# A table that places the maxima pieces inside each step of a four-stage transformer kernel

## The reference, cut to what matters

```python
scores = jnp.einsum('bhqd,bhkd->bhqk', query, key) / np.sqrt(D_K)      # 16 heads, 512 x 1601
scores = jnp.where(mask == 0, jnp.float32(-1000000000.0), scores)
attn = jax.nn.softmax(scores, axis=-1)
x = jnp.einsum('bhqk,bhkd->bhqd', attn, value)
```

## Time and profile before

| | |
|---|---|
| median of 3 runs | 2892.51 us (2891.18 to 2892.61) |
| profiled execution, span from the first to the last instruction | 2889.1 us |
| what the median has beyond that span | 3.4 us |
| TensorE busy by the profile | 2692.4 us, 93% |
| VectorE busy | 1738.0 us, 60% |
| ScalarE busy | 1458.0 us, 50% |
| mean granted clock of TensorE | 0.985 |

### The profile page before, as it was taken

One profiled execution on the slowest core, in us unless ns is written; L12 is line 12 of the kernel. 1 busy time (PEld: TensorE's weight loads), 2 busy tenths in 40 slices (PEclk: granted clock), 3 DMA queues, 4 the chain that ended last, 5 costly groups with the idle time before them and its releaser, 6 DMA issues.

```text
span 2889.1 us, 39579 instructions
## 1 busy us (share of the span) xinstructions
PE 2692.4 (93%) x13707; PEld 1286.5 (45%) x13707; DVE 1738.0 (60%) x4231; ACT 1458.0 (50%) x2923; POOL 281.4 (10%) x344
## 2 busy tenths in 40 slices
PE   7878999999999999999999999999999989879998
PEld 3533433343334433443334343533353323239998
DVE  3346676667766776577666766676666768641111
ACT  2232565546554656456545755565546556633332
POOL 1200200010001100020002000200010000002222
PEclk8988999999999999999999999999999999999999
DMA  5431312323132313241224032422322032039995
GB/s 180 124 102 42 100 42 77 91 76 81 32 108 75 100 41 108 53 121 42 88 56 131 18 107 60 107 50 68 99 62 63 18 83 47 10 115 369 375 375 208
DMA packets 215141, 296.37 MB, mean 103 GB/s; under 512 B 50533, under 2 KB 180813, under 8 KB 214934
## 3 DMA queue, kind: packets, MB, share of 16 engines
q1 hardware_dynamic: 198428, 221.50, 27.3%
q0 software_dynamic: 16512, 72.32, 7.3%
HBM read 232.87 MB, written 60.50 MB: 102 GB/s over the span
## 4 chain that ended last, share of the span: by engine, by line
PE 79%; DVE 8%; ACT 6%; issue 5%; DMA 2%; SPq 1%; POOL 0%; ACTq 0%; POOLq 0%; DVEq 0%
PE PS L1462 12%; PE PS L1418 11%; PE PS L1445 10%; PE PS L1104 6%; DVE mxC L1984 6%; PE PS L1079 6%; PE PS L1644 5%; PE PS L1656 5%; PE PS L1133 3%; PE PS L1306 3%; PE PS L1200 2%; ACT reg L970 2%; PE PS L1223 2%; PE PS L1092 2%; PE PS L1215 2%
## 5 line engine op out<-in xcount | busy, mean ns | idle before, releaser
L970 ACT ACTIVATE reg<-PS 128x512 f32<-128x512 f32 (+1 forms) x1664 | 971.9, 598 | 962.5 <-PE PS L1445 956.8
L1984 DVE TENSOR_REDUCE mxC<-PS 128x1 f32<-128x400 f32 (+1 forms) x2048 | 1097.1, 570 | 560.8 <-PE PS L1418 548.0
L1418 PE MATMUL PS<-reg 96*128 96x400 bf16 (+1 forms) x2048 | 669.1, 340 | 64.2 <-DVE mxC L1984 39.4
L1445 PE MATMUL PS<-reg 99*128 99x512 bf16 (+1 forms) x1664 | 613.1, 384 | 38.0 <-ACT reg L970 29.5
L1418 PEld LDWEIGHTS PS<-reg 96*128 96x128 bf16 x2048 | 194.7, 97 | 585.2 <-DVE mxC L1984 452.4
L1462 PE MATMUL PS<-reg 128*17 128x512 f32 (+1 forms) x3328 | 440.0, 601 | 0.3 <-DVE reg L2008 0.3
L1445 PEld LDWEIGHTS PS<-reg 99*128 99x128 bf16 (+1 forms) x1664 | 163.2, 100 | 383.7 <-ACT reg L970 237.4
L1104 PE MATMUL PS<-reg 128*128 128x512 f32 (+1 forms) x416 | 211.6, 601 | 0.4 <-ACT reg L844 0.4
L1079 PE MATMUL PS<-reg 128*128 128x512 f32 (+1 forms) x512 | 208.8, 522 | 1.0 <-ACT reg L871 0.7
L1016 ACT ACTIVATE reg<-PS,reg 128x128 f32<-128x128 f32 x312 | 89.3, 369 | 217.3 <-PE PS L1644 217.3
L1644 PEld LDWEIGHTS PS<-reg 128*128 128x128 f32 x1248 | 147.8, 194 | 3.1 <-issue 1.0
(11 more groups left out here) (233 smaller groups left out, 2552.9 us busy)
## 6 DMA issues: line engine op xcount, KB each, us to landing
reg<-in_D_W SPq DMA_DIRECT2D x78, 1024.0 KB, 9.3
reg<-in_A_mask POOLq DMA_DIRECT2D x32, 800.5 KB, 5.7
dramK<-reg SPq DMA_DIRECT2D x144, 100.0 KB
dramV<-reg SPq DMA_DIRECT2D x48, 272.0 KB, 3.1
reg<-in_ctxT POOLq DMA_DIRECT2D x8, 1601.0 KB, 8.8
reg<-in_ctx POOLq DMA_DIRECT2D x8, 1536.0 KB, 7.7
dramQ<-reg SPq DMA_DIRECT2D x96, 128.0 KB
reg<-dramQ SPq DMA_DIRECT2D x32, 384.0 KB, 6.4
```

The lines of the kernel that those rows point to most:

```text
L970: act.activation(pr[u % RING][0:r, :], PS[0:r, s_bank(v), :], ACT.Exp).then_inc(a_expC, 1)
L1418: last = mm(PS[:, bank, 0:w], qs[(NG * bb + g) % 3][0:ROWS, h, t * P:(t + 1) * P], ks[g % 2][0:ROWS, h, c0:c0 + w], start=True, stop=True)
L1445: last = mm(PS[0:r, bank, :], ks[g % 2][0:STK, h, c * P:c * P + r], qs[(NG * b + g) % 3][0:STK, h, :], start=True, stop=not with_mask)
L1984: v.tensor_reduce(mxC[:, h, t, j:j + 1], PS[:, m_ring(bb, g)[i % len(m_ring(bb, g))], 0:M_CH[j][1]], AX.X, ALU.max).then_inc(v_mx, 1)
```

## The change

The table of four rows becomes one of four periods: batch 0, batches 1 to 5, batch 6, batch 7. Each has a row for each group, and an entry for each step. The digits of an entry say how many pieces `piece()` issues at its first, second, third call in the step. On VectorE the number of pieces in a step follows the new table, but `piece()` there still takes one at each call. All groups now begin in step 3, group 3 among them; the last piece lies in step 43 or 44. 64 pieces for each group, their order and their banks stay.

```diff
-PIECES = ("0001212322232223211111210112221321001111113300000000",
-          "0002203232320132102231233322111111031002110100000000",
-          "0001001211031002110222133323330021330113312300000000",
-          "0000000000032223311121332223311121221122211320000000")
+PIECES = (
...
+    ("0 0 0 1 01 11 01 011 1 01 101 012 0 0111 01 111 011 01 11 011 01 1 01 011 1 0 0 01 1 011 1 11 011 011 101 02 011 0 011 01 111 0 11 11 0111 0 0 0 0 0 0 0",
+     "0 0 0 1 021 1 011 02 01 1 011 11 0 1 012 01 112 0 021 02 012 0 021 02 021 01 0 111 1 1 0 02 01 1 1 02 1 01 1 11 01 0 11 021 0 0 0 0 0 0 0 0",
+     "0 0 0 11 02 0 01 02 01 1 1 011 0 11 01 02 01 0 0 111 0 01 0 11 021 111 1 01 111 111 1 01 111 1 012 01 1 012 0 02 111 1 01 0121 1 0 0 0 0 0 0 0",
+     "0 0 0 1 022 0 01 11 0 1 0211 02 01 012 01 02 021 1 001 02 0 0 112 11 01 111 11 01 112 0 1 11 0 1 01 02 01 0 1 11 1 0 0 112 02 0 0 0 0 0 0 0"),
...
+     "0 0 0 1 0 3 0 13 1 1 0 13 1 1 0 13 1 1 1 03 1 1 1 03 1 1 1 03 1 1 1 04 0 1 1 13 0 1 1 13 0 1 1 13 1 0 0 0 0 0 0 0"),
...
+def period(b):
+
+    return {0: 0, B - 2: 2, B - 1: 3}.get(b, 1)
+
+
+def slots(b, g, v):
+
+    return [int(d) for d in PIECES[period(b)][g].split()[v]]
+
+
+def chunks(b, g, v):
+
+    upto = [sum(int(d) for step in PIECES[period(b)][g].split()[:w] for d in step) for w in (v, v + 1)]
     return range(*upto)
...
                 g, v = u // UN, u % UN
                 if g < NG - 1:
-                    return (b, g + 1, chunks(g, v)) if 0 <= b < B else (b, g + 1, ())
-                return (b + 1, 0, chunks(g, v)) if 0 <= b + 1 < B else (b + 1, 0, ())
+                    return b, g + 1, chunks(b, g, v)
+                return (b + 1, 0, chunks(b, g, v)) if b + 1 < B else (b + 1, 0, ())
...
-                todo = iter(ahead)
+                todo, counts = iter(ahead), iter(slots(b, g, v))
 
                 def piece():
-                    for i in todo:
-                        scores_c(nb, ng, i, with_mask)
-                        break
+                    for _ in range(next(counts, 0)):
+                        scores_c(nb, ng, next(todo), with_mask)
```

More of the change, by code:

```diff
@@ L60 @@
 MT = (47, 46, 47, 47)
-PIECES = ("0001212322232223211111210112221321001111113300000000",
-          "0002203232320132102231233322111111031002110100000000",
-          "0001001211031002110222133323330021330113312300000000",
-          "0000000000032223311121332223311121221122211320000000")
+PIECES = (
[16 rows of a table added]
+)
 U_O1, U_O2, U_LD, U_XD, U_GATE = (8, 10), (13, 16), 18, (28, 30), 33
@@ L123, in rows @@
     return P if c < CT - 1 else CL
-def chunks(g, v):
-    upto = [sum(int(d) for d in PIECES[g][:w]) for w in (v, v + 1)]
+def period(b):
[4 more added lines that the diff above has]
+    upto = [sum(int(d) for step in PIECES[period(b)][g].split()[:w] for d in step) for w in (v, v + 1)]
     return range(*upto)
```

## The result

The changed kernel takes 2959.11 us (median of 4 runs, 2957.81 to 2960.84) against 2892.56 for the kernel before on the same chip: **slower, ratio 1.0232, 95% interval 1.0217 to 1.0246**, some 67 us. The forecast was 2922.5, its range ended at 2952, and the time lies above it. The profiled execution has a span of 2956.7 us, 67.6 more than before, so its stretches can be set against the rows of before directly. Lines of the code moved: on TensorE by 24 (`scores_c` is L1442, `scores_t` L1469, `transpose_m` L1456, `project_k` L1157), on VectorE by 23 (`maxima` is L2007), on GpSimd and SyncE by 24.

A forecast was written before the change was run, and what follows sets the result against it. TensorE was taken to bound the batches. Terms -10.0 + 2.5 + 1.7 + 8.8 + 2.2 = +5.2 us for each of batches 0 to 5, with batches 6 and 7 together +30: 2892.5 + 30 = 2922.5 us, range 2889 to 2952.

The forecast's parts named there:

- What bounds the kernel: Batches: TensorE, busy for 93% of the span; its waits are time, other engines' only if TensorE stands behind them.
- Group 3's stall: Group 3, step 3: the first piece waits 10.1 us for the next batch's queries; net +8.8 us a batch, 8.5 to 10.
- the path hangs on work ahead of step 155, which the change leaves alone: Queries' load in group 3: the landing stays some 14.1 us behind the group's start.
- The clock: TensorE behind group 3's stall: half clock for 4.0 to 8.8 us, losing 2.0 to 4.4; +2.2 us a batch taken.
- VectorE's order: VectorE's list: the prediction notes that reduces move between steps, and gives this no term in the sum.
- Pieces spread out: TensorE's pieces, all groups: two of one bank stay 1.0 us apart, so spreading gains 10.0 us a batch, 6.6 to 11.5.
- Short steps left bare: Steps with fewer pieces: waits ahead of `scores_t` grow from 3.0 to 5.3 us a batch; +2.5 taken, 0 to +4.
- the group's end: `transpose_m` waits for the split behind later last pieces: some 1.1 us in group 1, 0.6 in group 0; +1.7 a batch.
- Batches 6 and 7: Last two batches: batch 6 +1.1 us, its stall growing from 5.3 to some 10.7; batch 7 -2 us.
- The first: Rival, whole kernel: the pieces' waits outweigh stall and clock, 11.0 us a batch; not slower, 2867 at 14 us; chance 0.17.
- the pieces' bound: TensorE's pieces: the spread gains at most some 11.5 us a batch.
- The third: Rival, whole kernel: other waits take up every piece's wait, leaving the stall alone, +71 us, 2964; chance 0.06.

The follow-up runs named there:

- e3: The changed kernel with 32 matmuls, their product unused, on TensorE ahead of group 3's wait for the queries; ratio 1.0176 to the kernel before.
- e1: The changed kernel with the old counts in group 3, one piece at each place; groups 0 to 2 keep the new rows; ratio 1.0051 to the kernel before.
- e5: e1 with VectorE's reduces behind all its other work of their step, in all four groups; ratio 1.0009 to the kernel before.
- e6: e1 with the same number of pieces in every step, but one at each place from the first on; ratio 0.9968 to the kernel before.
- e12: e11 plus a group 3 row for batches 0 to 5, spread from step 11 by measured streaming time; ratio 0.9992 to the kernel before.
- e11: e6 with the old counts in batch 7; ratio 0.9952 to the kernel before.
- e10: The kernel before, with the mask load issued ahead of group 3's queries cut to 8 columns; 2880.2 us in a single run, 2891.6 before.

## Why the prediction was right, and where it failed

**What bounds the kernel**: right. By the profile 64 of the 67 us are TensorE's idle time; its busy time grew by 3 us, and that of VectorE and ScalarE fell.

**Group 3's stall**: right in kind, and near in size. The place, the idle first piece and its cause are as forecast, and e3 names the load. The step "the path hangs on work ahead of step 155, which the change leaves alone" was not quite true: a mask load on GpSimd's queue, which I had not listed among the things that stand behind the stall, moves behind the queries, and the stall is 8.1 us, not 10.1. Group 3 as a whole grew by 8.6 to 10.0 us in batches 0 to 3, by the forecast 9.0, but there the second fall of the clock is in it; in batches 4 and 5, without that, by 7.0 and 7.2. So that its +51.1 comes near the forecast +54 is in part luck: a stall that was shorter and a fall of the clock that was not in the sum.

**The clock**: right in kind. 2.2 us for each stall became 2.3, but a second fall behind 1.2 us of idle time, in four batches, was not in the sum; e3 measures 16 us for all of it, 13 forecast. The shorter time that the Trainium skill gives in "TensorE: Matmul & The Clock Gate", "HAM oscillation" (1.67 us throttled for each wait of its example) is not what the rows show: 4.6 us at half clock in batch 3.

**VectorE's order, priced at nothing: the step that failed.** The prediction notes "on VectorE it moves reduces between steps" and gives that no term. I laid out TensorE's list alone and held each piece to 1.0 us behind the one two before it, whatever VectorE was doing. But the diff names places on TensorE only, and VectorE goes through its list in the old order: a piece that TensorE makes late in its step stops what stands behind its reduce there, as `rest_k` at 1260.47. What that costs is the difference between e1 and e5, in which only VectorE's order differs: 23.1 us in groups 0 to 2 of batches 0 to 5, 3.9 a batch. With it gone these groups are 1.8 us a batch below before; with it they are 1.6 above in the changed kernel, where the forecast had -3.8. It shows as the waits ahead of `project_k`, `scores_t` and the transposes, which grew by more than the pieces' waits fell. e1 against e6 gives the same price from the other side: 24 us for naming the places. In e1 a part of it is the clock, which falls at the end of group 1 in four batches.

**Pieces spread out, -10.0 a batch: the size was wrong too.** From start to start (the distance to the matmul ahead less its streaming time) the pieces' waits in groups 0 to 2 of batch 3 fell by 3 to 4.5 us, by what is taken as the streaming time, where I had 6.5. VectorE's row had already shown a reduce held behind 0.68 us of other work; I used that to raise the upper bound of the gain, when it says as well that a piece's wait can outlast the 1.0 us of the laying out. In group 3 of the changed kernel, where the pieces had the steps from 3 on, the waits behind the stall's half clock went from 4.1 to 0.5 us, as laid out; in e12, evenly spread from step 11, they grew to 5.3, where laying out would have taken nearly all of them away.

**Short steps left bare, +2.5, and the group's end, +1.7**: right in kind, too large. The waits shown ahead of `scores_t` grew by 1.5 us in batch 3. At the end of group 1 the wait for the split was 0.67 (1.1 forecast), at the end of group 0 no such wait shows in batch 3 (0.6 forecast).

**Batches 6 and 7**: +7.6 and +1.4 in place of +1.1 and -2. In batch 6 the stall grew by 5.0 us (5.4 forecast), but its clock, priced at nothing because it fell already, stayed at 0.50 for 12.1 us behind the stall where it had 8.8; and groups 0 to 2, which were to gain, grew by 1.4 us. In batch 7 the waits for the split grew by 3.2 us for 1.2.

**The rivals.** The first, that the spread pays for the stall, needed more than the pieces' bound, and the opposite happened. The third, that the table does nothing so that the stall alone is left (2964), is the nearest to the measured time, but not its mechanism: the counts do gain 9 us or more (e6, e11), and the names lose more than that. The range took 6.6 us a batch as the least that the pieces could give; the sum around that bound had only TensorE's waits for reduces in it, and none for what VectorE makes others wait for.

## What to carry to other kernels

When two engines take turns on the same buffers, an order that is written for one of them has to be laid out for both: a producer that is moved later in its step makes the consumer wait in its own list, and everything behind it there. Read an experiment by stage before its total: e5 cured three groups and harmed the fourth, and its total showed half of the cure. Test counts and places one at a time: here the even counts gained 0.3 to 0.5% in three of four groups, while the places, with VectorE's list left as it was, cost 0.8% and the early start of the fourth group 1.9%. Before moving a consumer ahead of a load's landing, list what else on every queue moves behind the stall, since that changes the landing too.

## What the runs showed of the hardware that was not expected

A load of 384 KB in group 3 landed 4.8 to 5.8 us behind its issue when an 800 KB load of another queue was not issued just ahead of it (batches 0 to 5 of the changed kernel, and of e10 in one run), and 7.1 to 8.4 us when it was (the kernel before).

Single idle times of 1.0 to 1.3 us were followed by half clock for some 3.4 us in some batches and not in others. Behind the 1.22 us that begin at 1491.6 in the changed kernel the clock fell. Behind 1.05 us at the end of group 1 it fell in batches 2, 4 and 6 of the changed kernel, where another 0.67 us stood close behind; it did not fall there in its other batches, nor in any batch of the kernel before. What separates them these runs do not settle.

In e3, 7.07 us of matmuls whose product nobody reads cost nothing in batches 0 to 5, as TensorE stood still anyway, and gave back 16 us through the clock. In batch 6, where 4.23 us of idle time were left behind them, they gave nothing back.
